# Self and cross attention run as one pipeline of 64 sequences, and ACT copies the values ahead of the older pair's exponentials

## The reference

```python
h = _ln(x, g1, be1)
x = _attn(h, h, Wq1, Wk1, Wv1, Wo1, bo1) + x
h = _ln(x, g2, be2)
x = _attn(h, context, Wq2, Wk2, Wv2, Wo2, bo2) + x
h = _ln(x, g3, be3)
y = h @ Wp + bp
a, gate = (y[..., :FF_HID], y[..., FF_HID:])
x = a * jax.nn.gelu(gate, approximate=False) @ W2 + b2 + x
```

## Time and profile before

| | us or share |
|---|---|
| median of 3 runs (3154.82 to 3159.67) | 3159.18 |
| the profiled execution | 3161.7 |
| its span | 3159.9 |
| granted TensorE clock, mean | 0.99 |
| PE matmul busy | 2997.0 (95%) |
| PE weight load busy | 2595.8 (82%) |
| DVE busy | 2302.1 (73%) |
| ACT busy | 1879.8 (59%) |
| POOL busy | 1407.4 (45%) |
| DMA, mean rate | 198 GB/s |
| idle time of PE before self attention's transposes, ended by the copy of values | 0.3 |
| idle time of PE before cross attention's matmuls of Wq, ended by DVE's low parts | 5.7 |

### The profile page before, as it was taken

One profiled execution on the slowest core, in us unless ns is written; L12 is line 12 of the kernel. 1 busy time (PEld: TensorE's weight loads), 2 busy tenths in 40 slices (PEclk: granted clock), 3 DMA queues, 4 the chain that ended last, 5 costly groups with the idle time before them and its releaser, 6 DMA issues. The chain is left out here.

```text
span 3159.9 us, 77497 instructions
## 1 busy us (share of the span) xinstructions
PE 2997.0 (95%) x25600; PEld 2595.8 (82%) x25600; DVE 2302.1 (73%) x3851; ACT 1879.8 (59%) x5615; POOL 1407.4 (45%) x977
## 2 busy tenths in 40 slices
PE   7999999999999998699999999999999969999999
PEld 6888888888888887588888888888888758888888
DVE  6777777777777776587788777878887755555654
ACT  6666666666666665466666666666666632322232
POOL 5555555555555554455555555555555420001100
PEclk9999999999999999899999999999999989999999
DMA  8777788778787777588888878888888750000000
GB/s 253 235 236 234 233 239 236 233 236 242 237 240 238 236 239 225 173 241 240 239 243 248 240 238 240 242 241 244 240 244 239 229 145 27 27 27 33 33 27 21
DMA packets 464424, 625.01 MB, mean 198 GB/s; under 512 B 57728, under 2 KB 397056, under 8 KB 464128
## 3 DMA queue, kind: packets, MB, share of 16 engines
q1 hardware_dynamic: 460256, 624.09, 66.2%
q10 hardware_dynamic: 4128, 0.41, 0.1%
HBM read 330.71 MB, written 293.60 MB: 198 GB/s over the span
## 5 line engine op out<-in xcount | busy, mean ns | idle before, releaser
L382 POOL TENSOR_TENSOR self_probs<-self_probs,self_row_inv 128x1024 f32<-128x1024 f32 x256 | 484.8, 1894 | 578.2 <-DVE self_row_inv L576 575.4
L382 POOL TENSOR_TENSOR cross_probs<-cross_probs,cross_row_inv 128x1024 f32<-128x1024 f32 x256 | 484.8, 1894 | 565.3 <-DVE cross_row_inv L576 565.3
L429 ACT ACTIVATE cross_probs<-cross_ps_s,cross_neg_max 128x256 f32<-128x256 f32 x1024 | 474.5, 472 | 198.3 <-DVE cross_blocks L568 134.2
L429 ACT ACTIVATE self_probs<-self_ps_s,self_neg_max 128x256 f32<-128x256 f32 x1024 | 474.4, 472 | 121.8 <-DVE self_blocks L568 76.6
L549 DVE TENSOR_REDUCE self_neg_max<-self_ps_s 128x2 f32<-128x512 f32 x512 | 328.8, 684 | 170.2 <-PE self_ps_s L719 170.2
L549 DVE TENSOR_REDUCE cross_neg_max<-cross_ps_s 128x2 f32<-128x512 f32 x512 | 331.6, 684 | 135.0 <-PE cross_ps_s L719 134.0
L568 DVE STREAM_TRANSPOSE cross_blocks<-cross_probs 128x1024 f32<-128x1024 f32 x256 | 315.4, 1232 | 10.3 <-DMA cross_turns<-cross_blocks 9.4
L568 DVE STREAM_TRANSPOSE self_blocks<-self_probs 128x1024 f32<-128x1024 f32 x256 | 315.0, 1231 | 1.0 <-POOL self_probs L382 1.0
L738 PE MATMUL self_ps_o<-self_probs_t,self_v 128*64 128x256 f32 x2048 | 258.3, 388 | 30.4 <-DMA self_probs_t<-self_turns 30.2
L738 PE MATMUL cross_ps_o<-cross_probs_t,cross_v 128*64 128x256 f32 x2048 | 257.7, 389 | 27.2 <-DMA cross_probs_t<-cross_turns 26.8
L481 ACT ACTIVATE self_qk_hi<-self_ps_qk 128x512 fp32r<-128x512 f32 x256 | 153.2, 599 | 213.4 <-PE self_ps_s L719 114.3
(11 more groups left out here) (170 smaller groups left out, 9623.8 us busy)
## 6 DMA issues: line engine op xcount, KB each, us to landing
self_turns<-self_blocks SPq DMA_DIRECT2D x1024, 128.0 KB, 2.8
self_probs_t<-self_turns SPq DMA_DIRECT2D x256, 512.0 KB, 4.3
cross_turns<-cross_blocks SPq DMA_DIRECT2D x1024, 128.0 KB, 2.9
cross_probs_t<-cross_turns SPq DMA_DIRECT2D x256, 512.0 KB, 4.3
self_xt<-in_x SPq DMA_DIRECT2D x32, 256.0 KB, 6.3
self_xres<-in_x SPq DMA_DIRECT2D x32, 256.0 KB, 2.7
after_self_attention<-yout SPq DMA_DIRECT2D x32, 256.0 KB, 2.4
cross_xt<-after_self_attention SPq DMA_DIRECT2D x32, 256.0 KB, 6.4
```

Of the source, the lines that this page charges most:

```text
L382: pool.tensor_tensor(tile, tile, scale, ALU.mult).then_inc(probs_ready, 1)
L429: last = act.activation(probs[:, slot % 2, h, t], scores[:, slot % 2, h, t], ACT.Exp, bias=neg_max[:, slot % 2, i:i + 1], accum_out=row_su ...
```

## The change

Both attentions become one call over 64 sequences. A sequence has a part and a stage, SELF or CROSS: sequence 0 is FIRST, 1 stands alone as straight code, 2 to 30 are a loop, 31 is LAST of SELF, 32 is SEAM, 33 to 62 are a second loop, 63 is LAST of CROSS, and one DRAIN follows. LAST of SELF does the work ahead (load, statistics, transposes of x and of the context) for sequence 32, and SEAM finishes the pairs of self attention with self attention's Wo while it starts cross attention's own.

The weights sit in two sets of buffers, where the raw values and the low part are one buffer (split in place). Cross attention's weights are split inside self attention: ACT makes the high parts of Wq and Wk at the end of steps 0 and 2 of sequence 1, DVE the low part of Wq and POOL that of Wk in step 4; the same for Wv (DVE) and Wo (POOL) in sequence 31. The feed-forward weights are loaded in step 2 of SEAM and split in the DRAIN of cross, and `feed_forward` no longer splits them.

In every step ACT copies the values (`copy_v`) right behind the high parts of pair g, ahead of the exponentials of pair g-2; before, it came behind them.

Beside these: six loads of constants on ACT's queue in front of one loop, one yout buffer in place of two, one counter of stores for both attentions, and a wait per weight on PE.

```diff
--- before.py
+++ after.py
@@ sequences @@
-    for p in range(0, PAIRS, 2):
-        step(0, p, FIRST)
-    with nc.Fori(1, n - 1, engines=[eng.engine], hint_back_edge=True) as b:
+    def sequence(b, part, stage):
         for p in range(0, PAIRS, 2):
-            step(b, p, LOOP)
-    for p in range(0, PAIRS, 2):
-        step(n - 1, p, LAST)
+            step(b, p, part, stage)
+
+    sequence(0, FIRST, SELF)
+    sequence(1, LOOP, SELF)
+    with nc.Fori(2, n - 1, engines=[eng.engine], hint_back_edge=True) as b:
+        sequence(b, LOOP, SELF)
+    sequence(n - 1, LAST, SELF)
+    sequence(n, SEAM, CROSS)
+    with nc.Fori(n + 1, 2 * n - 1, engines=[eng.engine], hint_back_edge=True) as b:
+        sequence(b, LOOP, CROSS)
+    sequence(2 * n - 1, LAST, CROSS)
     for p in range(0, PROJECTED, 2):
-        step(n, p, DRAIN)
+        step(2 * n, p, DRAIN, CROSS)
+
+
+def ahead(part, stage):
+
+    return part in (FIRST, LOOP, SEAM) or part == LAST and stage == SELF
@@ class AttentionWeights @@
+    def split_high(self, act, w):
+        act.wait_ge(self.loaded[w], self.count(w))
+        act.activation(self.hi(w), self.raw(w), ACT.Copy,
+                       scale=SCALE if w == "wq" else 1.0).then_inc(self.hi_ready[w], 1)
+
+    def split_low(self, eng, w):
+        eng.wait_ge(self.hi_ready[w], 1)
...
@@ SP, step @@
                 if part == FIRST and p == 2:
-                    prefetch(sp)
-                if part in (LOOP, LAST) and p == 6:
-                    store(b - 1)
+                    weights[CROSS].load(sp)
+                if part == SEAM and p == 2:
+                    sp.wait_ge(v_done, PAIRS // 2 * n)
+                    sp.wait_ge(qk_done, PAIRS * n)
+                    ff_w.load(sp)
+                if part in (LOOP, LAST, SEAM) and p == 6:
+                    store(b - 1, stage_behind(part, stage))
                     sp.wait_ge(y_stored, 16 * b)
-                    load_residual(b)
...
@@ POOL, step @@
+                if second(b, stage) and p == 4:
+                    weights[CROSS].split_low(pool, "wk")
+                if part == LAST and stage == SELF and p == 4:
+                    weights[CROSS].split_low(pool, "wo")
...
+                if part == DRAIN and p in (2, 4):
+                    for i in (p - 1, p):
+                        ff_w.split_low(pool, i)
@@ ACT, step @@
                 if part != DRAIN:
                     high_parts(g, p)
+                    copy_v(b, p)
                 if alive(part, p, EXPS):
                     for h in range(2):
                         exps(g - EXPS, (p - EXPS) % RING, h)
                 if part != DRAIN:
-                    copy_v(b, p)
-                    if part in (FIRST, LOOP) and p == TURN_H:
-                        scale_shift(b + 1)
-                    if part in (FIRST, LOOP) and p == 6:
+                    if ahead(part, stage) and p == TURN_H:
+                        scale_shift(b + 1, stage_ahead(part, stage))
+                    if ahead(part, stage) and p == 6:
                         high_h(b + 1)
...
+                if second(b, stage) and p in (0, 2):
+                    weights[CROSS].split_high(act, WEIGHTS[p // 2])
+                if part == LAST and stage == SELF and p in (0, 2):
+                    weights[CROSS].split_high(act, WEIGHTS[2 + p // 2])
+                if part == DRAIN and p < 6:
+                    for i in ((0,), (1, 2), (3, 4))[p // 2]:
+                        ff_w.split_high(act, i)
@@ DVE, step @@
+                if second(b, stage) and p == 4:
+                    weights[CROSS].split_low(nc.vector, "wq")
+                if part == LAST and stage == SELF and p == 4:
+                    weights[CROSS].split_low(nc.vector, "wv")
+                if part == DRAIN and p == 0:
+                    ff_w.split_low(nc.vector, 0)
...
```

More of the change, by code:

```diff
@@ L58 @@
 V_COLS = INNER // 4
-FIRST, LOOP, LAST, DRAIN = range(4)
+FIRST, LOOP, LAST, DRAIN, SEAM = range(5)
+SELF, CROSS = range(2)
 def counts(c):
@@ L140, in attention @@
[L140 to L146 removed]
+    def split_high(self, act, w):
[4 more added lines that the diff above has]
+        eng.wait_ge(self.hi_ready[w], 1)
+        if w == "wq":
+            eng.scalar_tensor_tensor(self.lo(w), self.raw(w), SCALE, self.hi(w).bitcast(F32),
+                                     ALU.mult, ALU.subtract).then_inc(self.lo_ready[w], 1)
+        else:
+            eng.tensor_tensor(self.lo(w), self.raw(w), self.hi(w).bitcast(F32),
+                              ALU.subtract).then_inc(self.lo_ready[w], 1)
@@ L148, in attention @@
+def attention(nc, tag, x_in, ctx_in, x_out, weights, bo, gamma, beta, ff_w, y_stored):
+    n = x_in[SELF].shape[0]
     with ExitStack() as es:
@@ L309, in load_turn, with step @@
                              ).then_inc(turn_loaded[slot % RING], 16)
-            def step(b, p, part):
+            def step(b, p, part, stage):
                 for pair in (p, p + 1):
@@ L314, in step @@
                         load_turn(b, pair)
-                if part in (FIRST, LOOP) and p == 0:
-                    load_next(b + 1)
+                if ahead(part, stage) and p == 0:
+                    load_next(b + 1, stage_ahead(part, stage))
                 for pair in (p, p + 1):
@@ L600, in step @@
                     inverse(b, p + 1)
-                if part in (FIRST, LOOP) and p == 2:
+                if ahead(part, stage) and p == 2:
                     norm_stats(b + 1)
@@ L657, in project_pair, with project_v @@
                 return last
-            def project_v(b, p, part):
+            def project_v(b, p, part, stage):
                 quarter = p // 2
@@ L1158, in block_program @@
-        feed_forward(nc, "ff_", x2, out, ff_w, w["bp"], w["b2"], w["g3"], w["be3"], stored[1])
+        w_split = []
+        for i in range(2):
+            with nc.sbuf_tensor(f"w_raw{i}", [P, len(WEIGHTS) * W_COLS], F32) as w_raw:
+                pass
+            w_lo = es.enter_context(nc.sbuf_tensor(f"w_lo{i}", [P, len(WEIGHTS) * W_COLS], F32R))
+            w_hi = es.enter_context(nc.sbuf_tensor(f"w_hi{i}", [P, len(WEIGHTS) * W_COLS], F32R))
+            w_split.append((w_hi, w_lo, w_raw))
```

349 lines of the change are left out of this document (171 added, 178 removed).

## The result

The changed kernel takes 3111.37 us, median of four runs (3104.96 to 3116.79); the kernel before 3157.0 over four runs (3153.57 to 3159.67). The ratio is 0.9853 with a 95% interval of 0.9834 to 0.9873, so 46 us are gained. Forecast were 54, and a time of 3105.1 in a range of 3090 to 3133. A later series gave 0.9863 (0.9843 to 0.9882).

A forecast was written before the change was run, and what follows sets the result against it. PE's own stream, busy 95% of the span, was taken to set the pace, leaving its gaps to win. Terms -39.3 + 1.2 + 7 + 4 - 27 = -54.1 off 3159.18 gave 3105.1 us, range 3090 to 3133.

The forecast's parts named there:

- A: Seam between self and cross attention: 78.4 us become one cross sequence of 39.1 with the pipeline full, -39.3 us.
- B: Work ahead in sequence 31: two more sets of four transposes at some 0.6 us each, +1.2 us.
- D: Feed-forward weights queued on SP before step 4's turned probabilities in SEAM: +4 us, bounds 0 and 12.
- C: Cross weights' splits inside self attention, sequences 1 and 31, on ACT, DVE and POOL: +7 us, from 2 to 14.
- E: Copy of values moved ahead: cross attention's transposes stop waiting for ACT, -27 us, between -16.6 and -30.1; self attention unchanged.
- I add 1.2 for each: Within C: DVE's and POOL's splits overlapping in step 4, 1.2 us for each of the two, 2.4 together.
- The prediction's 14: Upper value of C: where POOL issues first, DVE stands still up to 4.6 us, 3.4 more twice.
- the slack of 1.0: Self attention: 1.0 us left between the exponentials pushed by the moved copy and PE's scores, so the copy costs nothing.
- F: Small things: three more constant loads at the start, a counter for all six, splits moved to DRAIN: 0, bound 3.
- R1: Rival, chance 0.20: PE waits for DVE's low parts before the scores instead of the copy; E is 0, 3132.1 us.
- R3: Rival, chance 0.04: ACT's exponentials become the bound in both attentions; at 0.4 us a step, 3206 us.
- R2: Rival, chance 0.12: splits and the weight load collide in full; C is 14 and D 12, 3120.1 us.

The follow-up runs named there:

- the repeated run: The changed kernel measured once more, as it is, beside three other runs on one chip: 3117.74 us, ratio 0.9863 to the kernel before.

## Why the prediction was right, and where it was off

**A, the seam: right in kind.** From sequence 30 to 33 the transposes gained 27.0, where A, B, D and sequence 31's half of C made -30.6. Some 2 of the 27.0 are E's, since two cross sequences lie in that stretch, so A's group made about 25. PE works through the seam. What was not in the sum is the clock. In SEAM and in the last self sequence it fell for a while after PE's waits: 1.7 us in SEAM, and 3.4 in the last self sequence, where 1.7 were lost before. That names 3.4 of the 5.6 missing. Before, the clock was low in the seam too, and for longer (0.50 from 1276 to 1300), and that time is in the 78.4.

**B** can't be told apart from the rest.

**C, the splits: right in sum, in part by luck.** The sum had 7; the medians with and without splits differ by 8.5, and PE's waits for the output's low part, which are absent without splits, sum to 6.75 (0.52, 0.53, 2.28 in sequence 1, and 1.13, 2.29 in sequence 31). Wrong was "I add 1.2 for each": the two rows of a partial overlap gave 0.4 for DVE, and what counts is who comes second. DVE came second and took 1.75 more. The slack, taken as 1.0, was larger by nearly as much (4.04 of split made 2.28 of wait, so 1.76), so 2.28 came out where 1.3 + 1.2 = 2.5 was taken. The Trainium skill, "SBUF — State Buffer", section "Who interferes with whom", says that the second of the two engines is blocked until the first has done its instruction. The durations bear that out within 0.2 us. The prediction's 14 by that rule was too much all the same, since POOL's split began 2.7 us before DVE's and only the rest of its time was lost. ACT's parts, taken as 0.5 four times, are the 0.52 and 0.53 in sequence 1 and the 1.13 in sequence 31.

**D, the load: +4 taken, 3.4 + 0.6 measured, and 1.7 more by the clock.** In the other seven profiles with this load on SP the first wait was 3.2 to 6.5, and 5.27 in the repeated run of the same kernel, so +4 is at the low side of what was seen. The bound of 0 is out, that of 12 was not reached.

**E, the copy: right.** -27 forecast; 28 by two pairs of ratios, and 31 by the pace. What it rested on held: the slack of 1.0, self attention's pace unchanged within 0.1 us, and no wait for DVE in the place of the copy's. The row to go by was the weight loads' 30.1, not the matmuls' 16.6: part of the wait stands in front of the weight loads, which come first.

**F, small things: this is the term that was off.** Its 0, with a bound of 3, was 3.5 by the first matmul alone, and the whole start lost 14.5 where C's half and F made 3.5. The prediction named the counter that waits for all six and gave no row for its 0; but such a counter makes the first consumer wait for the slowest, the broadcast of bo, which lands 12.2 us after issue where it had taken 9.5. Of the 14.5, 10.9 have a name: these 3.5, C's first half (3.3), the DMA wait at the loop's first turn (2.33) and the clock behind it (1.7), and the sum had neither of the last two. Another 2.8 were lost inside sequence 0, from its first matmul to its transposes of the next x (23.8 in place of 21.05). The copy alone makes 0.6 of that in the old kernel; the rest is open. The other side of F was right: the splits moved to the DRAIN cost the feed-forward stage nothing that can be told. Its first gate matmul comes 103.2 us after the last of the transposes above, at 2547.56, and came 102.9 after it before, at 2592.84.

R1 is out (the waits didn't come back elsewhere), R3 is out (one more copy costs nothing that can be told). R2 was half there: its lock and the queue's order were real and their prices smaller.

## What to carry to other kernels

Where two stages of one shape follow one another, run them as one pipeline; but count what the seam's work does where it goes: a split or a load that was free in a drain now stands in the queue of an engine that others wait for. Put such work where the other engine of the pair is idle, and try a large load on a queue that nobody waits for. Ahead of a copy that frees a bank, ask what the engine was waiting for anyway: a hole of one copy's length in front of the next instruction makes the move free. Give each consumer a counter of its own loads, the first one above all.

## What the runs showed of the hardware

- A DVE tensor operation with two inputs in SBUF that is issued while POOL's split or layer norm runs waits for the rest of POOL's instruction: 4.04 and 4.06 us for 2.29 of work, with 1.90 and 1.91 left of POOL's, and 2.05 for 1.22 of work, with 0.98 left.
- A wait of PE can cost more than its length. Behind the DMA wait of 2.33 in the changed kernel, and behind the wait of 2.28 for the output's low part at 89.13 in the repeated run, the granted clock was at its lower level (1.2 in place of 2.4 GHz) for a stretch that cost 1.7 us by the windows; other stretches cost twice that. It did not follow each such wait: behind the 2.29 at 1263.24 the clock stayed at 1.00.
- With 3 MB of weights on ACT's queue PE waited 1.86 us for turned probabilities in that step and 2.32 later, with the same 3 MB ahead on SP's own queue 3.2 to 6.5 in that step.
